# Scaling of normed tokens on ScalarE instead of VectorE, in a one-core macaron block

## The chip, the cores and the metric

The kernel runs on one core of a Trainium2 chip. The metric is device time in microseconds of one execution, given as the median of several runs; smaller is better.

## The reference

`x` has 4 batches of 512 tokens with 128 features. Three residual stages follow one another, each behind a layer norm over the 128 features:

```python
def _layernorm(x, axis=-1, eps=1e-05):
    m = jnp.mean(x, axis=axis, keepdims=True)
    v = jnp.var(x, axis=axis, keepdims=True)
    return (x - m) / jnp.sqrt(v + eps)

x = x + 0.5 * ffn(_layernorm(x), gate_w, Wg, Wu, Wd)
x = x + attn(_layernorm(x), Wa, ba, We, be, Wi, Wo, Wv, Wout, chi, beta_p, iv_p, ov_p)
x = x + 0.5 * ffn(_layernorm(x), gate_w, Wg, Wu, Wd)
```

`ffn` is a mixture of 8 experts in which every expert picks its 128 best tokens of a batch by a softmax over the gate logits; `attn` has 16 heads of 8 features, a softmax over the scores, and gates from two further projections of the normed tokens. Everything is float32.

## The kernel before

Tokens lie on the 128 partitions. `x` and `xn` hold 16 tiles of 128 tokens by 128 features: a batch `b` is 4 such tiles (`C = 4`, `B = 4`). The program is written by hand, one instruction queue for each engine; the order inside a queue is the order of the code, and engines release one another only by semaphores. An engine whose next instruction waits does nothing that stands behind it.

All three norms use the same parts, numbered `n` = 0, 1, 2. For each batch:

- VectorE, `norm_stats(n, b)`: four `bn_stats` and four `bn_aggr` give mean and variance of each token.
- ScalarE, `root(n, b)`: one square root of the four variances of each partition, with `norm_eps` as its bias, a tile of one column.
- VectorE, `norm_apply(n, b)`: one reciprocal (`rstd`), a wait for it, and four `tensor_scalar` that subtract the mean and multiply by `rstd` (L640).
- TensorE, `turn_xn(n, b)`: four transposes of `xn` into a PSUM bank (L956), each waiting for its own tile.
- ScalarE, `copy_xnT(n, b)`: one copy of that bank to `xnT` (L498).

In norm 0 VectorE does the statistics of batch `b` before `norm_apply` of batch `b - 1`. TensorE turns batch `b` and then makes the gate logits of batch `b - 1` (L963); `route` needs all four. GpSimd splits every `xn` batch in two float16 halves (L424, L426) for the gathers of the expert stages, in norms 0 and 2.

In norm 1 TensorE's order is: turn batch 0, `project_qk(0)` (L1103), turn batches 1 and 2, `project_vae(0)` (L1116), `project_qk(1)`, `project_vae(1)`, turn batch 3, `project_qk(2)`, `project_vae(2)`, and from there the row maxima of the scores (L1136, L810). The result of `project_qk` is kept as a high part, rounded by ScalarE (`copy_qk_hi`, L566), and a low part, the rest, by VectorE (`split_qk_lo`, L831). Both are stored to DRAM by SyncE (`store_parts`, L328) and loaded again as stacks (L335). There are two buffers of the parts, so batch `b` waits until the stores of batch `b - 2` have landed: ScalarE for the high ones, VectorE for the low ones. ScalarE's queue is `root(1, 0)`, `copy_xnT(1, 0)`, `root(1, 1)`, `copy_qk_hi(0)`, `root(1, 2)`, `copy_xnT(1, 1)`, `copy_xnT(1, 2)`, `root(1, 3)`, `copy_qk_hi(1)`, `copy_xnT(1, 3)`, `copy_qk_hi(2)` and so on. VectorE also adds the expert output to `x` (`add_moe`, L803) and the bias to the other projections (`add_bias`, L838).

In norm 2, the last heads of the attention are finished between the batches. TensorE's order is `turn_heads`, `turn_xn(2, 0)`, `turn_combined(3)`, `project_out(3)`, `turn_xn(2, 1)`, `logits(1, 0)` (which also waits for `x_attended`), `turn_xn(2, 2)`, `logits(1, 1)`, `turn_xn(2, 3)`, `logits(1, 2)`, `logits(1, 3)`.

Of the kernel before, what the change touches and what calls it, by code (L numbers as in the profile page):

```python
# [11 lines left out]
P = 128  # L12
F32 = mybir.dt.float32
# [5 lines left out]
ALU = mybir.AluOpType  # L19
ACT = mybir.ActivationFunctionType  # L20
# [27 lines left out]
def macaron_block(nc, x_in, Wa, ba, We, be, Wi, Wo, Wv, Wout, chi, beta_p, iv_p, ov_p, gate_w, Wg, Wu, Wd, out):  # L48
    B, S, D = x_in.shape
    H = Wa.shape[1]  # L50
    DH = D // H
    E, _, I = Wg.shape
    K = max(1, int(S / E * 2))
    C = S // P
    CL = C // 2
    T = B * C
# [13 lines left out]
    with ExitStack() as ctx:  # L70
        def sb(name, shape, dt=F32):
            return ctx.enter_context(nc.sbuf_tensor(name, shape, dt))
# [26 lines left out]
        x = sb("x", [P, T, D])  # L99
        xn = sb("xn", [P, T, D])  # L100
# [5 lines left out]
        mean_var = sb("mean_var", [P, T, 2])  # L106
        std = sb("std", [P, T])
        rstd = sb("rstd", [P, T])

        top = sb("top", [P, T])  # L110

# [81 lines left out]
        def by(n, name):  # L193
            return [sem(f"{name}{i}") for i in range(n)]


        dve_norm, var_ready, std_ready = by(3, "dve_norm"), by(3, "var_ready"), by(3, "std_ready")
        xn_ready, xn_turned, xnT_ready = by(3, "xn_ready"), by(3, "xn_turned"), by(3, "xnT_ready")

        pool_halves, halves_ready = by(2, "pool_halves"), by(2, "halves_ready")  # L200
# [21 lines left out]

        qk_projected, qk_hi_ready, qk_lo_ready = sem("qk_projected"), sem("qk_hi_ready"), sem("qk_lo_ready")

        hi_stored, lo_stored = ([by(2, f"{name}_stored{u}_") for u in range(2)] for name in ("hi", "lo"))
        vae_projected, vae_ready = sem("vae_projected"), sem("vae_ready")
        gate_exp_ready, gate_one_ready, gates_ready = sem("gate_exp_ready"), sem("gate_one_ready"), sem("gates_ready")
        swap_ready, wout_swapped, dve_rot, act_rot, rot_ready = (
# [56 lines left out]
        def _(sp):  # L285
# [34 lines left out]

            load_experts(0)
            def store_parts(b):
                for half, (parts, ready, stored) in enumerate(((part_hi, qk_hi_ready, hi_stored), (part_lo, qk_lo_ready, lo_stored))):
                    for qk in range(2):
                        blocks = parts_dram[qk, b].rearrange("h d (m n) t -> m n (h d) t", m=2)
                        sp.wait_ge(ready, 2 * b + qk + 1)
                        twice = blocks[half] if qk == 0 else blocks[:, half]
                        sp.dma_start(twice.rearrange("n r t -> r n t"),  # L328
                                     parts[:, b % 2, qk, :].bitcast(F32).unsqueeze(1).broadcast_to([P, 2, S])).then_inc(stored[b % 2][qk], 16)

            def load_stacks(b, g):
                for qk, stack in enumerate((q_stack, k_stack)):
# [17 lines left out]
                             k_rows_dram).then_inc(k_rows_filled, 16)  # L350
            store_parts(0)
            for qk in range(2):
                sp.wait_ge(hi_stored[0][qk], 16)
                sp.wait_ge(lo_stored[0][qk], 16)
            load_stacks(0, 0)
            store_parts(1)
            for g in range(1, G):
# [5 lines left out]
            load_max_rows(1, 1)  # L363
            for u in range(2):
                for qk in range(2):
                    sp.wait_ge(hi_stored[u][qk], 16 * B // 2)
                    sp.wait_ge(lo_stored[u][qk], 16 * B // 2)
            with sp.Fori(0, B - 1) as b:
                for step in range(1, G + 1):
                    n = b * G + step  # L370
# [119 lines left out]
        def _(act):  # L490
            def root(n, b):
                t = slice(b * C, (b + 1) * C)
                act.wait_ge(var_ready[n], C * (b + 1))
                nc.scalar.activation(std[:, t], mean_var[:, t, 1], ACT.Sqrt, bias=norm_eps[:]).then_inc(std_ready[n], 1)

            def copy_xnT(n, b):
                act.wait_ge(xn_turned[n], b + 1)
                nc.scalar.copy(xnT[:, b, :], ps[:, b, :]).then_inc(xnT_ready[n], 1)  # L498
# [53 lines left out]
            act.wait_ge(eps_made, 1)  # L552
            root(0, 0)
            for b in range(B):
                if b < B - 1:
                    root(0, b + 1)
                copy_xnT(0, b)
# [3 lines left out]
            def copy_qk_hi(b):  # L561
                for qk in range(2):
                    act.wait_ge(qk_projected, 2 * b + qk + 1)
                    if b >= 2:
                        act.wait_ge(hi_stored[b % 2][qk], 16 * (b // 2))
                    nc.scalar.copy(part_hi[:, b % 2, qk, :], ps[:, 4 + qk, :]).then_inc(qk_hi_ready, 1)  # L566

            def copy_max_rows(n, slot):
# [1 line left out]
                nc.scalar.copy(max_rows[:, slot, :], ps[0:HG * C, 7, 0:P]).then_inc(max_rows_ready, 1)  # L570

            root(1, 0)
            copy_xnT(1, 0)
            root(1, 1)
            copy_qk_hi(0)
            root(1, 2)
            copy_xnT(1, 1)
            copy_xnT(1, 2)
            root(1, 3)
            copy_qk_hi(1)  # L580
            copy_xnT(1, 3)
            copy_qk_hi(2)
# [5 lines left out]
            def copy_heads(n, slot):  # L588
                act.wait_ge(probs_used, n * C + 2 * C)
                act.wait_ge(heads_turned, n + 1)  # L590
                nc.scalar.copy(heads_out[:, slot, :], ps[:, 6, :]).then_inc(heads_copied, 1)
# [20 lines left out]
            for b in range(B - 1):  # L612
                root(2, b)
            copy_heads(B * G - 1, 1)
            copy_xnT(2, 0)
            copy_xnT(2, 1)
            root(2, B - 1)
            copy_xnT(2, 2)
            copy_xnT(2, 3)
            route(1)  # L620
            experts(1)
# [3 lines left out]
        def _(dve):  # L625
# [5 lines left out]
                for t in tiles:  # L631
                    nc.vector.bn_aggr(out=mean_var[:, t, :], in_=stats[:, t, :]).then_inc(var_ready[n], 1)

            def norm_apply(n, b, steps):
                t0 = slice(b * C, (b + 1) * C)
                dve.wait_ge(std_ready[n], b + 1)
                steps.did(nc.vector.reciprocal(rstd[:, t0], std[:, t0]))
                steps.settle()
                for t in range(b * C, (b + 1) * C):
                    nc.vector.tensor_scalar(xn[:, t, :], x[:, t, :], mean_var[:, t, 0:1], rstd[:, t:t + 1],  # L640
                                            ALU.subtract, ALU.mult).then_inc(xn_ready[n], 1)

            def rotation_angles(steps):

# [172 lines left out]
            for b in range(B):  # L817
                dve.wait_ge(x_loaded[b], 16)
                norm_stats(0, b, steps)
                if b > 0:  # L820
                    norm_apply(0, b - 1, steps)
            norm_apply(0, B - 1, steps)
            route(0)
            experts(0)

            def split_qk_lo(b):
                for qk in range(2):
                    dve.wait_ge(qk_hi_ready, 2 * b + qk + 1)
                    if b >= 2:
                        dve.wait_ge(lo_stored[b % 2][qk], 16 * (b // 2))  # L830
                    nc.vector.tensor_tensor(part_lo[:, b % 2, qk, :], ps[:, 4 + qk, :], part_hi[:, b % 2, qk, :].bitcast(F32),  # L831
                                            ALU.subtract).then_inc(qk_lo_ready, 1)

# [9 lines left out]
            for b in range(B):  # L843
                dve.wait_ge(x_added[0], b + 1)
                norm_stats(1, b, steps)
                if b < B - 1:
                    add_moe(0, b + 1)
                    norm_apply(1, b, steps)
                if b == B - 2:
                    split_qk_lo(0)  # L850
            norm_apply(1, B - 1, steps)
            dve.wait_ge(attention_consts, 1)
            add_bias(0)
            split_qk_lo(1)
# [77 lines left out]
            copy_combined(2)  # L932
            add_attention(2)
            norm_heads(B - 1, 2, steps)
            norm_apply(2, 0, norm_steps)
            norm_heads(B - 1, 3, steps)
            copy_combined(3)
            norm_apply(2, 1, norm_steps)
            add_attention(3)
            norm_apply(2, 2, norm_steps)  # L940
            norm_apply(2, 3, norm_steps)
            route(1)
            experts(1)
            for b in range(B):
# [344 lines left out]
```

## Time and profile before

| | |
|---|---|
| median of 3 runs | 482.74 us (482.29 to 483.13) |
| profiled execution, its own time | 482.52 us |
| its span in the profile | 480.8 us |
| TensorE matmul busy | 397.7 us, 83% |
| VectorE busy | 385.2 us, 80% |
| ScalarE busy | 232.2 us, 48% |
| GpSimd busy | 54.5 us, 11% |
| chain that ended last | TensorE 64%, VectorE 16%, ScalarE 4% |

The span leaves out 1.7 us around the profiled execution's work. Busy shares are averages over stages that have different limits: the three norms lie at about 4 to 20 us, 125 to 146 us and 355 to 372 us of the span, and what the change does is decided in those stretches.

### The profile page before, as it was taken

How to read it: one execution, taken by the hardware profiler on the slowest of the kernel's cores; microseconds unless marked ns; L12 is line 12 of the kernel's file. 1: busy time of each engine (PE TensorE's matmuls, PEld its weight loads, DVE VectorE, ACT ScalarE, POOL GpSimd, SP SyncE). 2: the span in 40 equal slices, each digit the busy share in tenths (PEclk: the TensorE clock that was granted, in tenths of full speed). 3: DMA queues.
4: the chain of work that ended last, by engine and by line, in shares of the span. 5: the costliest groups of instructions: out<-in, count | busy, mean ns of one | idle time of the engine just before them, and what ended most of it. 6: DMA issues, size and time to landing. Idle time of an engine off the chain costs nothing.

```text
span 480.8 us, 7695 instructions
## 1 busy us (share of the span) xinstructions
PE 397.7 (83%) x2204; PEld 213.2 (44%) x2204; DVE 385.2 (80%) x841; ACT 232.2 (48%) x439; POOL 54.5 (11%) x103
## 2 busy tenths in 40 slices
PE   2702999999778889999999999999977019999995
PEld 1600456776543543333333333334427004567764
DVE  6698957788789888999898899987546889577883
ACT  2400453432341157777777777778863003543322
POOL 4520002122000010000000000000014400011210
PEclk9999999999897669999999999999996558999998
DMA  6100002223069721111112111100200000022103
GB/s 178 46 0 0 1 1 67 65 58 92 4 237 287 274 79 46 45 46 46 44 49 56 60 49 52 44 1 2 67 1 0 0 1 1 1 65 65 41 25 89
DMA packets 25767, 27.48 MB, mean 57 GB/s; under 512 B 3920, under 2 KB 17488, under 8 KB 25680
## 3 DMA queue, kind: packets, MB, share of 16 engines
q1 hardware_dynamic: 25744, 27.20, 18.6%
q8 instruction: 12, 0.20, 0.2%
q14 instruction: 11, 0.09, 0.1%
HBM read 17.08 MB, written 9.98 MB: 56 GB/s over the span
## 4 chain that ended last, share of the span: by engine, by line
PE 64%; DVE 16%; issue 12%; ACT 4%; POOL 1%; DMA 1%; DVEq 0%; ACTq 0%; POOLq 0%
PE ps L1151 14%; PE ps L1161 13%; PE ps L1136 6%; PE ps L1038 5%; DVE probs L748 4%; DVE neg_max L810 3%; PE ps L1021 3%; PE ps L1053 3%; PE ps L1023 3%; PE ps L1054 3%; PE ps L1022 3%; ACT probs L599 2%; PE ps L963 2%; PE ps L1170 2%; DVE heads_out L709 2%
## 5 line engine op out<-in xcount | busy, mean ns | idle before, releaser
L810 DVE TENSOR_REDUCE neg_max<-ps 128x1 f32<-128x512 f32 x256 | 161.1, 681 | 14.3 <-PE ps L1136 14.2
L599 ACT ACTIVATE probs<-ps 128x512 f32<-128x512 f32 x256 | 136.8, 601 | 44.0 <-PE ps L1151 42.8
L1136 PE MATMUL ps<-stacks 63*128 63x512 f32 x256 | 105.7, 494 | 3.3 <-DVE neg_max L810 2.6
L1151 PE MATMUL ps<-stacks 64*128 64x512 f32 x256 | 95.0, 462 | 4.9 <-ACT probs L599 4.8
L1151 PEld LDWEIGHTS ps<-stacks 64*128 64x128 f32 x256 | 41.3, 190 | 76.3 <-ACT probs L599 65.7
L1161 PE MATMUL ps<-probs,v_ext 128*32 128x512 f32 x512 | 69.0, 612 | 0.0
L1136 PEld LDWEIGHTS ps<-stacks 63*128 63x128 f32 x256 | 43.8, 196 | 19.5 <-DVE neg_max L810 15.0
L525 ACT CAST stacks<-ps 128x512 fp32r<-128x512 f32 x32 | 17.2, 588 | 67.5 <-PE ps L1002 67.5
L771 DVE TENSOR_TENSOR vae_and_gates<-heads_out,ps 128x512 f32<-128x512 f32 x32 | 21.9, 686 | 21.3 <-ACT heads_out L533 19.3
L453 POOL TENSOR_TENSOR w_lo<-w_gu,w_hi 128x512 fp32r<-128x512 f32 x16 | 20.6, 1295 | 150.1 <-ACT w_hi L512 150.1
L748 DVE TENSOR_TENSOR probs<-slot_row,slot 128x1024 f16<-128x1024 f16 x32 | 36.5, 1219 | 0.1
L1002 PE MATMUL ps<-probs,xn_hi 128*128 128x512 f16 x64 | 26.2, 410 | 7.4 <-DVE probs L748 6.7
L537 ACT COPY down_out<-ps 128x512 f32<-128x512 f32 x16 | 9.4, 587 | 45.8 <-PE ps L1038 45.8
L1021 PE MATMUL ps<-stacks,w_hi 128*128 (+1 forms) x64 | 30.4, 475 | 1.1 <-ACT stacks L525 0.8
L1038 PE MATMUL ps<-vae_and_gates,wd_sb 128*128 128x512 f32 x64 | 30.5, 598 | 0.8 <-DVE vae_and_gates L771 0.8
L977 PE MATMUL ps<-ident,threshold_row 32*128 32x32 f32 x2 | 0.6, 310 | 33.4 <-DVE threshold_row L718 33.4
L478 POOL TENSOR_TENSOR v_ext<-vae_and_gates,expression 128x128 f32 (+1 forms) x16 | 6.5, 409 | 190.8 <-PE ps L1161 132.8
L763 DVE TENSOR_SCALAR place<-token_row,indexT 128x512 fp32r<-128x512 f32 x64 | 27.9, 499 | 0.0
L1053 PE MATMUL ps<-place,part_hi 128*128 128x512 f32 x64 | 26.5, 413 | 0.4 <-DVE part_hi L785 0.4
L533 ACT ACTIVATE heads_out<-ps 128x512 f32<-128x512 f32 x32 | 19.1, 598 | 15.3 <-PE ps L1023 13.6
L1002 PE MATMUL ps<-probs,xn_lo 128*128 128x512 f16 x64 | 26.3, 411 | 0.0
L1023 PE MATMUL ps<-stacks,w_lo 128*128 (+1 forms) x64 | 25.2, 394 | 0.0
(150 smaller groups left out, 539.2 us busy)
## 6 DMA issues: line engine op xcount, KB each, us to landing
stacks<-parts_dram SPq DMA_DIRECT2D x64, 128.0 KB, 2.4
parts_dram<-part_hi SPq DMA_DIRECT2D x8, 512.0 KB, 3.5
parts_dram<-part_lo SPq DMA_DIRECT2D x8, 512.0 KB, 5.8
w_gu<-in_L_ffn_Wg_dram SPq DMA_DIRECT2D x16, 128.0 KB, 2.1
w_gu<-in_L_ffn_Wu_dram SPq DMA_DIRECT2D x16, 128.0 KB, 2.2
wd_sb<-in_L_ffn_Wd_dram SPq DMA_DIRECT2D x16, 128.0 KB, 2.2
x<-in_L_attn_x_dram SPq DMA_DIRECT2D x4, 256.0 KB, 3.7
stacks<-k_rows_dram SPq DMA_DIRECT2D x2, 512.0 KB, 6.6
```

The costliest lines, as they stand in the source:

```text
L599: nc.scalar.activation(probs[:, u // HG, u % HG, :], ps[:, RING + ring_bank(step, u), :], ACT.Exp, scale=SCORE_SCALE).then_inc(probs_ready, 1)
L748: nc.vector.tensor_tensor(pick[:, b, c], slot_row[:].unsqueeze(1).broadcast_to([P, E, K]), slot[:, c, b * E:(b + 1) * E].unsqueeze(2).broa ...
L763: nc.vector.tensor_scalar(place[:, u, b, :], token_row[:], indexT[:, b, bass.ds(2 * i + o, 1)], None, ALU.is_equal).then_inc(place_ready[l ...
L810: nc.vector.tensor_reduce(neg_max[:, g, col, qt:qt + 1], ps[:, ring_bank(step, u), :], AX.X, ALU.max, negate=True).then_inc(max_taken, 1)
L1002: last = nc.tensor.matmul(ps[:, pick_bank(n) + k, :], half[:, C * b + c, :], pick[:, b, c, 4 * hf:4 * hf + 4, :], start=(c == 0), stop=(c ...
L1021: nc.tensor.matmul(ps[:, bank, :], w_hi[:, u, k, cols], tokens_hi, start=True, stop=False)
L1023: nc.tensor.matmul(ps[:, bank, :], w_lo[:, u, k, cols], tokens_hi, start=False, stop=True).then_inc(gate_up_done[l], 1)
L1038: last = nc.tensor.matmul(ps[:, 6, :], wd_sb[:, u, m, :], hidden[:, u, m, :], start=(m == 0), stop=(m == MI - 1))
L1053: nc.tensor.matmul(ps[:, b, :], wy_hi[:, u, b, :], place[:, u, b, :], start=False, stop=False, skip_group_check=True)
L1136: nc.tensor.matmul(ps[:, ring_bank(step, u), :], q_stack[rows, g, pp, chunk(qt)], k_stack[rows, g, pp, :], start=True, stop=True).then_inc ...
L1151: nc.tensor.matmul(ps[:, RING + ring_bank(step, u), :], k_stack[rows, g, pp, chunk(c)], q_stack[rows, g, pp, :], start=True, stop=True).th ...
L1161: last = nc.tensor.matmul(ps[32 * j:32 * j + 32, 6, :], v_ext[:, g, c, j, :], probs[:, c, j, :], start=(c == 0), stop=(c == C - 1))
```

## The change

VectorE's `norm_apply` becomes `norm_scale`: after the reciprocal, one small instruction makes `shift = -mean * rstd` for the four tiles of the batch. ScalarE's new `normalise(n, b)` then makes each tile as `rstd * x + shift`, with both as per-partition operands. `normalise` gets a place in ScalarE's queue in each norm, and some roots and copies there change places with it. Apart from that, the store of the high part and that of the low part of one buffer count on one semaphore, so that both must have landed before either part is written again, and SyncE waits once where it waited twice.

```diff
+        shift = sb("shift", [P, T])
...
+        scales_ready = by(3, "scales_ready")
...
-        hi_stored, lo_stored = ([by(2, f"{name}_stored{u}_") for u in range(2)] for name in ("hi", "lo"))
+        parts_stored = [by(2, f"parts_stored{u}_") for u in range(2)]
...
             for qk in range(2):
-                sp.wait_ge(hi_stored[0][qk], 16)
-                sp.wait_ge(lo_stored[0][qk], 16)
+                sp.wait_ge(parts_stored[0][qk], 32)
...
+            def normalise(n, b):
+                act.wait_ge(scales_ready[n], b + 1)
+                for t in range(b * C, (b + 1) * C):
+                    nc.scalar.activation(xn[:, t, :], x[:, t, :], ACT.Identity, bias=shift[:, t:t + 1],
+                                         scale=rstd[:, t:t + 1]).then_inc(xn_ready[n], 1)
...
             root(0, 0)
             for b in range(B):
+                normalise(0, b)
                 if b < B - 1:
                     root(0, b + 1)
                 copy_xnT(0, b)
...
                     if b >= 2:
-                        act.wait_ge(hi_stored[b % 2][qk], 16 * (b // 2))
+                        act.wait_ge(parts_stored[b % 2][qk], 32 * (b // 2))
                     nc.scalar.copy(part_hi[:, b % 2, qk, :], ps[:, 4 + qk, :]).then_inc(qk_hi_ready, 1)
...
             root(1, 0)
+            normalise(1, 0)
+            root(1, 1)
             copy_xnT(1, 0)
-            root(1, 1)
+            normalise(1, 1)
             copy_qk_hi(0)
             root(1, 2)
             copy_xnT(1, 1)
+            normalise(1, 2)
+            root(1, 3)
             copy_xnT(1, 2)
-            root(1, 3)
+            normalise(1, 3)
             copy_qk_hi(1)
             copy_xnT(1, 3)
             copy_qk_hi(2)
...
             copy_heads(B * G - 1, 1)
+            normalise(2, 0)
+            normalise(2, 1)
             copy_xnT(2, 0)
+            normalise(2, 2)
             copy_xnT(2, 1)
             root(2, B - 1)
             copy_xnT(2, 2)
+            normalise(2, 3)
             copy_xnT(2, 3)
...
-            def norm_apply(n, b, steps):
+            def norm_scale(n, b, steps):
                 t0 = slice(b * C, (b + 1) * C)
                 dve.wait_ge(std_ready[n], b + 1)
                 steps.did(nc.vector.reciprocal(rstd[:, t0], std[:, t0]))
                 steps.settle()
-                for t in range(b * C, (b + 1) * C):
-                    nc.vector.tensor_scalar(xn[:, t, :], x[:, t, :], mean_var[:, t, 0:1], rstd[:, t:t + 1],
-                                            ALU.subtract, ALU.mult).then_inc(xn_ready[n], 1)
+                nc.vector.scalar_tensor_tensor(out=shift[:, t0], in0=mean_var[:, t0, 0], scalar=-1.0, in1=rstd[:, t0],
+                                               op0=ALU.mult, op1=ALU.mult).then_inc(scales_ready[n], 1)
...
                     if b >= 2:
-                        dve.wait_ge(lo_stored[b % 2][qk], 16 * (b // 2))
+                        dve.wait_ge(parts_stored[b % 2][qk], 32 * (b // 2))
```

Every call of `norm_apply` becomes one of `norm_scale` in the same place of VectorE's queue.

## Rows read from the trace of the kernel before

**Rows 1.** The page: busy time of each engine, and the chain by engine.

```profile
PE 397.7 (83%) x2204; PEld 213.2 (44%) x2204; DVE 385.2 (80%) x841; ACT 232.2 (48%) x439; POOL 54.5 (11%) x103
...
PE 64%; DVE 16%; issue 12%; ACT 4%; POOL 1%; DMA 1%; DVEq 0%; ACTq 0%; POOLq 0%
```

**Rows 2.** Instructions that write xn: durations in ns, minimum, median, maximum.

```profile
L640 DVE TENSOR_SCALAR xn<-x,mean_var,rstd x48: 333/341/1315, 7.1 to 367.3; 128x128 f32<-128x128 f32 x48
```

**Rows 3.** Timeline of norm 0: start, duration, engine, line.

```profile
6.85 0.18 DVE L637 RECIPROCAL rstd<-std 128x4 f32<-128x4 f32 x1 [0.54 <-ACT std L494]
7.06 1.12 DVE L640 TENSOR_SCALAR xn<-x,mean_var,rstd 128x128 f32<-128x128 f32 x4
...
8.75 0.58 ACT L498 COPY xnT<-ps 128x512 f32<-128x512 f32 x1 [1.74 <-PE ps L956]
...
13.84 2.38 DVE L640 TENSOR_SCALAR xn<-x,mean_var,rstd 128x128 f32<-128x128 f32 x4
...
14.28 0.58 ACT L498 COPY xnT<-ps 128x512 f32<-128x512 f32 x1 [1.80 <-PE ps L956]
14.47 1.16 POOL L426 TENSOR_TENSOR xn_lo<-xn,xn_hi 128x512 f16<-128x512 f32 x1
...
20.00 0.29 DVE L688 TENSOR_REDUCE top<-ps 128x16 f32<-128x128 f32 x1 [3.78 <-PE ps L963]
```

**Rows 4.** Timeline of ScalarE: activations back to back, without and with a per-partition bias.

```profile
20.65 0.31 ACT L516 ACTIVATE expo<-shifted 128x128 f32<-128x128 f32 x1 [1.98 <-DVE shifted L690]
20.87 0.19 ACT L502 ACTIVATE hp<-head_params 128x3 f32<-128x3 f32 x1
20.96 0.19 ACT L503 ACTIVATE hp<-head_params 128x1 f32<-128x1 f32 x1
...
356.31 0.67 ACT L494 ACTIVATE std<-mean_var,norm_eps 128x4 f32<-128x4 f32 x3
```

**Rows 5.** ScalarE's group of roots: busy us, mean ns of one, idle before.

```profile
L494 ACT ACTIVATE std<-mean_var,norm_eps 128x4 f32<-128x4 f32 x12 | 3.2, 293 | 3.3 <-DVE mean_var L632 3.2
```

**Rows 6.** Timeline of norm 1 and of the maxima behind it.

```profile
127.80 1.11 DVE L640 TENSOR_SCALAR xn<-x,mean_var,rstd 128x128 f32<-128x128 f32 x4
...
129.98 2.07 PE L1103 MATMUL ps<-xnT,wi_sb 128*128 128x512 f32 x2 [0.68 <-ACT xnT L498]
...
131.84 1.66 PE L1103 MATMUL ps<-xnT,wo_sb 128*128 128x512 f32 x2
...
134.57 1.12 DVE L640 TENSOR_SCALAR xn<-x,mean_var,rstd 128x128 f32<-128x128 f32 x4
...
138.66 1.11 DVE L640 TENSOR_SCALAR xn<-x,mean_var,rstd 128x128 f32<-128x128 f32 x4
139.69 0.88 DVE L838 TENSOR_TENSOR vae_and_gates<-ps,bias_row 128x320 f32<-128x320 f32 x2
...
140.32 1.32 PE L1116 MATMUL ps<-wvae_sb,xnT 128*128 128x160 f32 x8 [1.44 <-DVE vae_and_gates L838]
...
146.64 0.58 ACT L566 CAST part_hi<-ps 128x512 fp32r<-128x512 f32 x1 [2.22 <-PE ps L1103]
...
155.70 0.68 DVE L831 TENSOR_TENSOR part_lo<-ps,part_hi 128x512 fp32r<-128x512 f32 x1
```

**Rows 7.** Two stretches of norm 1: busy time by engine, granted clock, DMA.

```profile
132.00:133.00 1.00, 1.00 (x3) 0.41 (x2) 0.96 (x8) 0.58 (x1) 0.00 (x0) 0.50 0.00 0
133.00:134.00 1.00, 0.94 (x5) 0.36 (x3) 0.69 (x3) 0.46 (x1) 0.00 (x0) 0.94 0.38 141
```

**Rows 8.** Timeline of SyncE's queue in norm 1 and behind it.

```profile
140.59 1.78 SPq L335 DMA_DIRECT2D stacks<-parts_dram  x4
...
143.47 2.27 SPq L328 DMA_DIRECT2D parts_dram<-part_lo  x2
```

**Rows 9.** Timeline of norm 2.

```profile
363.99 1.11 DVE L640 TENSOR_SCALAR xn<-x,mean_var,rstd 128x128 f32<-128x128 f32 x4
...
365.23 2.38 DVE L640 TENSOR_SCALAR xn<-x,mean_var,rstd 128x128 f32<-128x128 f32 x4
```

More of the change, by code:

```diff
@@ L322, in store_parts @@
             def store_parts(b):
-                for half, (parts, ready, stored) in enumerate(((part_hi, qk_hi_ready, hi_stored), (part_lo, qk_lo_ready, lo_stored))):
+                for half, (parts, ready) in enumerate(((part_hi, qk_hi_ready), (part_lo, qk_lo_ready))):
                     for qk in range(2):
@@ L328, in store_parts @@
                         sp.dma_start(twice.rearrange("n r t -> r n t"),
-                                     parts[:, b % 2, qk, :].bitcast(F32).unsqueeze(1).broadcast_to([P, 2, S])).then_inc(stored[b % 2][qk], 16)
+                                     parts[:, b % 2, qk, :].bitcast(F32).unsqueeze(1).broadcast_to([P, 2, S])).then_inc(parts_stored[b % 2][qk], 16)
             def load_stacks(b, g):
@@ L365, in _ @@
                 for qk in range(2):
-                    sp.wait_ge(hi_stored[u][qk], 16 * B // 2)
-                    sp.wait_ge(lo_stored[u][qk], 16 * B // 2)
+                    sp.wait_ge(parts_stored[u][qk], 32 * B // 2)
             with sp.Fori(0, B - 1) as b:
@@ L820, in _ @@
                 if b > 0:
-                    norm_apply(0, b - 1, steps)
-            norm_apply(0, B - 1, steps)
+                    norm_scale(0, b - 1, steps)
+            norm_scale(0, B - 1, steps)
             route(0)
@@ L847, in _ @@
                     add_moe(0, b + 1)
-                    norm_apply(1, b, steps)
+                    norm_scale(1, b, steps)
                 if b == B - 2:
                     split_qk_lo(0)
-            norm_apply(1, B - 1, steps)
+            norm_scale(1, B - 1, steps)
             dve.wait_ge(attention_consts, 1)
@@ L934, in _ @@
             norm_heads(B - 1, 2, steps)
-            norm_apply(2, 0, norm_steps)
+            norm_scale(2, 0, norm_steps)
             norm_heads(B - 1, 3, steps)
             copy_combined(3)
-            norm_apply(2, 1, norm_steps)
+            norm_scale(2, 1, norm_steps)
             add_attention(3)
-            norm_apply(2, 2, norm_steps)
-            norm_apply(2, 3, norm_steps)
+            norm_scale(2, 2, norm_steps)
+            norm_scale(2, 3, norm_steps)
             route(1)
```

## The prediction, made blind

> **What bounds the kernel now.** I read the page first, for the shares and the chain of the work that ended last [rows 1]. TensorE is busy 83% and VectorE 80%, ScalarE 48%, which invites the thought that work should go from VectorE to ScalarE. The reader should not stop there: the chain is TensorE for 64% and the norms are a few short stretches in it. So I went to the instructions that write `xn`, 48 of them at a median of 0.341 us [rows 2], and to the timeline of the three norms, which shows what happens around each batch of four.
>
> In norm 0 the first batch of four takes 1.12 us on VectorE and its copy `xnT` starts at 8.75 [rows 3]. The last batch takes 2.38 us instead of 1.12: one of its four instructions is the one of 1.3 us [rows 2], and it stands beside GpSimd's subtraction at 14.47 [rows 3]. So before, `xn` is complete at 13.84 + 2.38 = 16.22 us. TensorE then ends the last turn and makes the last logits, and `route` begins on VectorE at 20.00, as soon as they are there [rows 3]. From 16.22 to 20.00 nothing has slack, and in all of norm 0 TensorE runs at the pace of the turns, which wait for `xn`.
>
> In norm 1 the start is a chain through all engines: `xn` of batch 0 from 127.80, its copy, then `project_qk(0)` at 129.98 [rows 6]. `xn` of batch 2 comes at 134.57 and ends at 135.69. At 140.32 comes a different limit: TensorE had idled 1.44 us for VectorE's bias add at 139.69, which was late because VectorE was making `xn` of batch 3 from 138.66 [rows 6]. This is the place where relief of VectorE can pay. In norm 2 batches 2 and 3 of `xn` are the chain: from 363.99 and from 365.23, the latter again 2.38 us long [rows 9].
>
> **The price of one instruction.** Before: 0.34 us each and 1.12 us for four, a pace of (1.12 - 0.34) / 3 = 0.26 us. After: a ScalarE activation of 128x128 with two per-partition operands, of which the trace has none. The nearest row is `expo`, 128x128 from SBUF with constants: 0.31 us, and the next activation begins 0.87 - 0.65 = 0.22 us after it; the tiny one behind lets the next begin after 0.09 us [rows 4]. Of the operands the only row is `root`, whose bias is per partition: 0.293 us for 4 columns [rows 5] against 0.19 us for the tiny one, and three take 0.67 us, so (0.67 - 0.29) / 2 = 0.19 us of pace against 0.09 [rows 4]. One such operand costs 0.10 us, in duration and in pace alike. The second (the scale) has no row. I take it to cost the same: both are one value per partition to be fetched before the stream begins. That makes 0.51 us for one, a pace of 0.42 at most; I use 0.50 and 0.40, so four take 3 x 0.40 + 0.50 = 1.70 us. The bounds: if neither operand costs anything with 128 columns, four take 3 x 0.22 + 0.31 = 0.97 us; if the second is free, 1.33 us; if the second costs twice the first, about 2.1 us. I call the duration of four q and keep it in the sums.
>
> The Trainium skill has a figure for this that the trace can be held against ("ScalarE: Activation LUTs", section "What ACT_TABLE_LOAD costs"): 186 ns with immediates plus 0.833 ns a column, about 93 ns more for each per-partition operand, and about 93 ns of overlap between neighbours. By that an estimate is 479 ns for one and 1.64 us for four; `expo` and `root` agree with it within 0.02 us. The same page's "Rules for kernel authors" say to use VectorE for adds and multiplies, which speaks against the change; by its figure the sum below would be about 0.35 us smaller.
>
> VectorE's part that stays is the reciprocal, 0.18 us [rows 3], and one new small instruction, which I take at the reciprocal's price, 0.20 us with its wait: `xn` starts 0.2 us later than it did.
>
> **Norm 0.** ScalarE now makes a ring with TensorE: four `xn`, then the turn, then the copy, then the next four. The copy began 0.57 us after the last `xn` (8.18 to 8.75) and holds the engine about 0.49 us before the next can begin (its 0.58 less the 0.09 of overlap) [rows 3, 4]; with 0.02 for the wait a batch takes q + 1.08 us. The first starts at 7.27, so `xn` of batch 3 is complete at 7.27 + 4q + 3 x 1.08 = 10.51 + 4q. With q = 1.70 this is 17.31 against 16.22, +1.09 us. `root` stands between `xn` and the copy and hides in the 0.57. The statistics on VectorE come earlier, which buys nothing, since the ring waits for its own engine. The stall beside GpSimd goes away (ScalarE's copy at 14.28 keeps its 0.58 us while GpSimd works from 14.47 [rows 3]), and it is counted: 16.22 contains it. The break-even is q = 1.43. Below about q = 1.3 TensorE's own work sets the end, about 1.9 us earlier than now.
>
> **Norm 1.** `xn` of batch 0 starts at 127.99 and ends 0.78 us later than it did (129.69 against 128.91), so `project_qk(0)` starts at 130.76. It runs at half clock; the granted clock is 0.50 until 133 and 0.94 in the next microsecond [rows 7]. If the clock rises when it did, the four matmuls end at about 133.65 against 133.50 (131.84 + 1.66 [rows 6]), if it rises 0.78 later, at 134.30; call this E. Behind it on ScalarE stand `copy_qk_hi`, the root, `copy_xnT(1, 1)`, 0.49 + 0.19 + 0.49 us and small waits, then `xn` of batch 2: it ends at E + 2.92, that is 136.57 to 137.22 against 135.69. The turn of batch 2, `project_vae(0)` and `project_qk(1)` follow and end at 139.8 to 140.4 where they ended at 138.9. There the idle time of 1.44 us is waiting to be used: VectorE, without its four `xn`, has the bias ready by about 139.2, so TensorE goes on at once, at 139.8 to 140.4 against 140.32. `copy_xnT(1, 2)`, which now stands behind a root that waits for statistics, is ready near 138.8 and is not needed before 141.6. So norm 1 loses 0.1 us or gains 0.6: the gain on VectorE pays for the loss on ScalarE. I take 0, as the clock more likely follows the work.
>
> **Norm 2.** `xn` of batch 2 can start only when VectorE has its statistics: 364.19 instead of 363.99. Behind it on ScalarE stand `copy_xnT(2, 1)` (0.49) and the last root (0.30), then on VectorE the reciprocal and the shift (0.4), so batch 3 starts at 365.30 + q and ends at 365.30 + 2q = 368.70 against 367.61 (365.23 + 2.38 [rows 9]): +1.09. The break-even is q = 1.16. `copy_xnT(2, 0)` now stands behind `xn` of batch 1 and makes the logits of batch 0 begin some 0.5 us later, but TensorE then waits for the turn of batch 2 anyway, which hides this. TensorE's turn of batch 0 now ends where the turn of the last heads begins, which costs 0.05 at most.
>
> **The semaphores.** `copy_qk_hi(2)` now also needs the low parts of batch 0. They have landed at 140.59, since the stacks' load, which waits for both, is issued then [rows 8], and the copy is not due before 143: nothing. `copy_qk_hi(3)` needs the low parts of batch 1, issued from 143.47 over 2.27 us [rows 8], where its projection ends at 146.6 [rows 6]. It may wait some microseconds, but what follows needs it only at 155.7, when VectorE comes to `split_qk_lo(3)` after 16 maxima [rows 6]: nothing. Fewer waits on SyncE: nothing.
>
> **Sum.** 1.09 + 0 + 1.09 = +2.18 us on the span of 480.8, and the same on that execution's own 482.52. The median of the runs is 482.74, 0.22 above it; I forecast 482.74 + 2.18 = 484.9 us. What a measurement of this kernel tells from no change is about 0.2%, 1.0 us.
>
> **The rivals.** *The operands are cheap (faster).* One mechanism: the fetch of the second operand hides behind the first, or that of both behind the stream. It decides at q = 1.43 in norm 0. With q = 1.33 norm 0 gives -0.4, norm 1 -0.8 (the bias wait is used up fully), norm 2 +0.3: 481.8 us. With q = 0.97: -1.9, -1.4, -0.45: 479.0 us. For it: no row shows two operands. Against it: the one row of one shows 0.10 us at full. Chances 0.12 and 0.04.
>
> *The clock comes earlier (about the same).* In norm 1 TensorE recovers at 133.1 whatever the work does; then norm 1 gives -0.6, and norm 2's clock, half from 365, may cost or return as much. About 483.8 us and less. For it: the edge falls 3 us after the work began; against: one edge proves no fixed time. Chance 0.13.
>
> *A late store, or a table to be loaded for the new function.* If the low store of batch 1 landed after 155.7, each microsecond past it would count: up to 487. If the new function needed a table of its own, every root and every batch behind it would need a load again, and a single load is longer than a norm batch's slack: about 10 us. Copies run behind the roots without one. Chance 0.05 together.
>
> **How the numbers follow.** The forecast's case has 0.66; its own range is 483.7 to 486.4 (norm 1 from -0.6 to +0.9, q from 1.6 to 1.8). Slower by over 0.2% (above 483.7): 0.60 of it, 0.05 of the clock's case, 0.05 of the last, 0.70. Within 0.2%: 0.05, 0.07 and half of the 0.12, 0.17 in round numbers. Faster: the other half, the 0.04 and what is left, 0.13. For 8 in 10 the range goes from the rival with one cheap operand to a q of 1.8: 481.7 to 486.4.
>
> **What would show it.** The activation group at 0.48 to 0.51 us, four in 1.6 to 1.7; `route` of norm 0 starting near 21.1 instead of 20.00; the wait of TensorE on the bias add gone from norm 1; the first reduction behind norm 2 about 2.2 us later. The forecast is wrong if four take less than 1.4 us, or if the clock's edges shift stretches that I took as fixed.

## The result: slower, by more than forecast

| | median of runs | ratio to before, 95% interval |
|---|---|---|
| before | 482.51 us (481.76 to 483.13, 4 runs) | |
| changed | 486.85 us (485.35 to 489.06, 4 runs) | 1.0094 (1.0052 to 1.0136) |
| changed, run again | 486.06 us (485.07 to 487.57, 6 runs) | 1.0075 (1.0053 to 1.0096) |

The forecast was 484.9 us, with a range up to 486.4. The direction was right; the loss is +3.6 to +4.3 us where +2.2 was forecast. A ratio compares an edited kernel with the kernel before as it ran beside it (17 to 23 executions, medians of 482.22 to 482.61 us, from the last row of the table on), so the medians of two experiments below can be compared only to some tenths of a microsecond. The profiled execution of the changed kernel is the quickest of its four: 485.35 us, with a span of 483.6 against 480.8. The page of the changed kernel, busy times and granted clock in tenths, where [rows 1] has the busy times of before; the clock line of before follows:

```profile
PE 401.9 (83%) x2204; PEld 213.7 (44%) x2204; DVE 372.5 (77%) x805; ACT 250.4 (52%) x487; POOL 54.5 (11%) x103
...
PEclk9999999999888569999999999999996558999999
```

```profile
PEclk9999999999897669999999999999996558999998
```

VectorE lost 12.7 us of work and ScalarE gained 18.2; the span grew by 2.8. The two new kinds of instruction, durations in ns (minimum, median, maximum):

```profile
L499 ACT ACTIVATE xn<-x,shift,rstd x48: 477/482/497, 7.2 to 370.0; 128x128 f32<-128x128 f32 x48
```

```profile
L654 DVE SCALAR_TENSOR_TENSOR shift<-mean_var,rstd x12: 161/172/1011, 7.0 to 367.8; 128x4 f32<-128x4 f32 x12
```

The activation is at the forecast price, 0.48 us against 0.50. The small instruction has a median of 0.17 and a maximum of 1.01 us: this is the first thing that was not forecast.

**Where the time went.** I cut each profile at the same events: the first statistics, the first reduction of routing 0 (`top`), the first add to `x` in norm 1, the first row maximum, the table load of norm 2, the reduction of routing 1. Each number is the difference of two starts in the timelines.

| stretch | before | changed | difference |
|---|---|---|---|
| norm 0, to `top` | 16.15 | 16.93 | +0.78 |
| routing and experts 0 | 105.10 | 105.00 | -0.10 |
| norm 1, to the first maximum | 20.76 | 21.04 | +0.28 |
| maxima and attention | 209.15 | 208.90 | -0.25 |
| norm 2, to `top` | 16.38 | 18.60 | +2.22 |

Norm 0, timeline of the changed kernel, for [rows 3]: four activations take 1.65 us, the copy follows, and the ring has a period of 2.70 us: the three batches behind the first start 2.70 us apart, and the last at 15.28.

```profile
7.18 1.65 ACT L499 ACTIVATE xn<-x,shift,rstd 128x128 f32<-128x128 f32 x4 [0.44 <-DVE shift L654]
...
9.39 0.58 ACT L504 COPY xnT<-ps 128x512 f32<-128x512 f32 x1 [0.38 <-PE ps L970]
...
15.28 1.65 ACT L499 ACTIVATE xn<-x,shift,rstd 128x128 f32<-128x128 f32 x4
...
20.70 0.29 DVE L702 TENSOR_REDUCE top<-ps 128x16 f32<-128x128 f32 x1 [5.79 <-PE ps L977]
```

Norm 2, timeline, for [rows 9]. The reader is to see the `shift` instructions beside GpSimd's subtractions: the first starts at 364.62, while the subtraction of 364.00 runs until 365.15, and ends at 365.17; the second starts at 367.77 and ends at 368.78, with GpSimd busy from 367.61 to 368.76. ScalarE starts its four only then. The reciprocal at 364.43, which reads one tile, takes its 0.15 us beside the same subtraction. In the kernel before, the table load starts at 355.01 and the reduction at 371.39 (the last line below, from its timeline).

```profile
364.00 1.15 POOL L426 TENSOR_TENSOR xn_lo<-xn,xn_hi 128x512 f16<-128x512 f32 x1
...
364.43 0.15 DVE L652 RECIPROCAL rstd<-std 128x4 f32<-128x4 f32 x1
364.62 0.55 DVE L654 SCALAR_TENSOR_TENSOR shift<-mean_var,rstd 128x4 f32<-128x4 f32 x1
365.20 1.65 ACT L499 ACTIVATE xn<-x,shift,rstd 128x128 f32<-128x128 f32 x4 [1.49 <-DVE shift L654]
...
367.61 1.15 POOL L426 TENSOR_TENSOR xn_lo<-xn,xn_hi 128x512 f16<-128x512 f32 x1
367.77 1.01 DVE L654 SCALAR_TENSOR_TENSOR shift<-mean_var,rstd 128x4 f32<-128x4 f32 x1
368.81 1.65 ACT L499 ACTIVATE xn<-x,shift,rstd 128x128 f32<-128x128 f32 x4 [0.81 <-DVE shift L654]
...
374.24 0.29 DVE L702 TENSOR_REDUCE top<-ps 128x16 f32<-128x128 f32 x1 [5.46 <-PE ps L977]
```

```profile
371.39 0.29 DVE L688 TENSOR_REDUCE top<-ps 128x16 f32<-128x128 f32 x1 [3.78 <-PE ps L963]
```

Norm 1, timeline, for [rows 6]. The bias add starts at 139.50, ahead of the end of `project_qk(1)`, and `project_vae(1)` follows at 141.28 with no wait for VectorE: that part of the plan works. But `project_qk(0)` takes from 131.44 to 135.23, and ScalarE waits 3.90 us for a store before it can write the high parts of batch 3 (and 2.02 us more for the second of them, at 151.82). The low parts that need them are made from 156.60 on, so this wait is hidden.

```profile
131.44 2.08 PE L1117 MATMUL ps<-xnT,wi_sb 128*128 128x512 f32 x2 [0.68 <-ACT xnT L504]
...
133.31 1.92 PE L1117 MATMUL ps<-xnT,wo_sb 128*128 128x512 f32 x2
...
139.50 0.89 DVE L852 TENSOR_TENSOR vae_and_gates<-ps,bias_row 128x320 f32<-128x320 f32 x2
...
141.28 1.25 PE L1130 MATMUL ps<-wvae_sb,xnT 128*128 128x160 f32 x8
...
149.21 0.58 ACT L573 CAST part_hi<-ps 128x512 fp32r<-128x512 f32 x1 [3.90 <-DMA parts_dram<-part_lo]
```

Windows of the same stretch; the number behind the five engines is the granted clock (0.50 is 1.2 GHz, 1.00 is 2.4). Before, it fell at 129.7 and was full again at 133.1 [rows 7]; here it fell at 130.0 and is half until 136.8. First two windows of the kernel before, then three of the changed one:

```profile
129.00:130.00 1.00, 0.33 (x3) 0.13 (x2) 0.97 (x8) 0.58 (x1) 0.00 (x0) 0.86 0.00 0
130.00:133.00 3.00, 3.00 (x4) 1.37 (x5) 2.93 (x16) 0.88 (x2) 0.00 (x0) 0.50 0.00 0
```

```profile
130.00:131.00 1.00, 0.77 (x2) 0.24 (x2) 0.83 (x5) 0.62 (x3) 0.00 (x0) 0.50 0.00 0
134.00:136.00 2.00, 2.00 (x6) 0.89 (x4) 0.00 (x0) 0.88 (x3) 0.00 (x0) 0.50 0.47 183
136.00:137.00 1.00, 0.08 (x1) 0.00 (x0) 0.89 (x4) 0.93 (x4) 0.00 (x0) 0.60 0.41 158
```

### The profile page after: what moved, and what is told of

Its sections match the earlier page's. It is cut to its first block, busy times and chain, and to the rows that moved or that the text cites. A ratio compares the mean times of both kernels' runs of the same rounds, so it can differ in the third digit from the quotient of the medians.

```text
span 483.6 us, 7704 instructions
## 1 busy us (share of the span) xinstructions
PE 401.9 (83%) x2204; PEld 213.7 (44%) x2204; DVE 372.5 (77%) x805; ACT 250.4 (52%) x487; POOL 54.5 (11%) x103
## 3 DMA queue, kind: packets, MB, share of 16 engines
q1 hardware_dynamic: 25744, 27.20, 18.2%
## 4 chain that ended last, share of the span: by engine, by line
PE 65%; DVE 14%; issue 12%; ACT 6%; POOL 1%; DMA 1%; DVEq 0%; ACTq 0%; POOLq 0%
PE ps L1165 14%; PE ps L1175 13%; PE ps L1150 6%; PE ps L1052 5%; DVE probs L762 4%; DVE neg_max L824 3%; PE ps L1067 3%; PE ps L1068 3%; PE ps L1035 3%; PE ps L1037 3%; PE ps L1036 3%; ACT probs L610 2%; PE ps L970 2%; PE ps L977 2%; PE ps L1117 2%
## 5 line engine op out<-in xcount | busy, mean ns | idle before, releaser
L610 ACT ACTIVATE probs<-ps 128x512 f32<-128x512 f32 x256 | 136.8, 601 | 43.8 <-PE ps L1165 42.6
L453 POOL TENSOR_TENSOR w_lo<-w_gu,w_hi 128x512 fp32r<-128x512 f32 x16 | 20.7, 1299 | 149.8 <-ACT w_hi L518 149.8
L970 PE MATMUL ps<-ident,xn 128*128 128x128 f32 x48 | 16.0, 404 | 13.7 <-ACT xn L499 13.1
```

What stands on the lines that cost most here:

```text
L610: nc.scalar.activation(probs[:, u // HG, u % HG, :], ps[:, RING + ring_bank(step, u), :], ACT.Exp, scale=SCORE_SCALE).then_inc(probs_ready, 1)
L970: last = nc.tensor.transpose(ps[:, b, chunk(c)], xn[:, C * b + c, :], ident[:])
```

## The experiments

Theory A: the loss beyond the forecast comes from two things, the `shift` stalled beside GpSimd in norm 2, and a longer half-clock time of TensorE in norm 1. The rivals: it is scatter of the runs; the shared semaphore; ScalarE's longer queue as such.

**The same kernel again.** No edit.

> The changed kernel once more, nothing edited. Theory A (the profile of the first execution, span +2.8 us, is the whole loss): most executions lie 2.5 to 3.5 us above the kernel before, and the first runs that were higher were scatter. Theory B (something that varies from execution to execution adds to it, most likely TensorE's clock coming back later in one stretch): the median is 4 to 5 us above, and a profile of a slow execution shows one stretch 1.5 us or more longer than in the first profile, at a lower granted clock.

Measured: 486.06 us, ratio 1.0075 (1.0053 to 1.0096), and a profile with the same stretches (norm 1 21.05, norm 2 18.58). The loss is not scatter. Which of the two theories holds is not decided: +3.6 us lies between them, and the profile is of one of the quicker executions. The three with a mean granted clock of 0.927 took 485.07 to 485.76 us, the two with 0.922 took 487.56 and 487.57; but one of the first four executions, also with 0.927, took 487.03, so the mean clock is not the whole of the scatter.

**The semaphore alone.** Of the diff only the `parts_stored` lines; all `norm_apply` as before.

> Only the shared semaphore of the stores of high and low parts; all norms scaled on VectorE as before. If the added wait is hidden, as forecast: 0 us, within 0.5. If ScalarE's wait for the low parts of batch 1 (it ended only at 151.8 us in the changed kernel's profile) is felt later, +1 to +2 us, with the maxima or the first attention step starting later.

Measured: 482.26 us, 0.9989 (0.9974 to 1.0003). The added wait is hidden.

**One norm at a time.** The lines of `normalise`, its order and `norm_scale` for one norm, the other two as before:

```diff
-            normalise(2, 0)
-            normalise(2, 1)
             copy_xnT(2, 0)
...
-            norm_scale(2, 0, norm_steps)
+            norm_apply(2, 0, norm_steps)
```

> Norm 0 alone on ScalarE (and the shared semaphore). From the profile of the changed kernel: the first reduction of the routing starts 0.7 to 0.8 us later, so +0.8 us in total. If the phase of TensorE's clock is what a shift in norm 0 disturbs in later stages, the total is 2 us or more, or scatters by more than 2 us from run to run.

> Norm 2 alone on ScalarE (and the shared semaphore). The working of the prediction gives +1.1 us. The theory formed from the changed kernel's profile (the small shift instruction on VectorE stands 0.4 and 0.85 us longer beside GpSimd's subtraction, and both stand in the chain) gives +2.2 us, with two shift instructions of 0.5 us or more.

> Norm 1 alone on ScalarE (and the shared semaphore). The forecast's working gives 0, from -0.6 to +0.1 us: the loss on ScalarE is paid by the wait of TensorE on the bias add. The remainder of the runs so far (3.6 for all three, less 0.9 and 2.6) says +0.1. If the changed order on ScalarE were a loss of its own, +1 us or more. In the profile the wait of TensorE on the bias add should be gone.

Measured: norm 0 483.74 us, 1.0019 (1.0006 to 1.0033), that is +0.9; norm 2 485.36 us, 1.0053 (1.0033 to 1.0073), +2.6; norm 1 484.18 us, 1.0031 (1.0019 to 1.0043), +1.5. Norm 2 has its `shift` instructions at 0.55 and 1.01 us again and takes 18.60 us. Norm 1, forecast at 0, costs: its profile has 22.05 us for the stretch, and two half-clock times in it, 130.5 to 133.9 and 137.4 to 140.8. Three of its windows:

```profile
131.00:133.00 2.00, 1.97 (x3) 0.94 (x4) 1.30 (x7) 1.52 (x4) 0.00 (x0) 0.50 0.00 0
134.00:137.00 3.00, 1.54 (x7) 0.64 (x5) 1.67 (x6) 2.52 (x7) 0.00 (x0) 1.00 0.66 256
137.50:140.50 3.00, 3.00 (x10) 2.65 (x11) 1.81 (x9) 2.39 (x6) 0.00 (x0) 0.50 0.97 376
```

The profiles of all experiments, those below included, can be set side by side for norm 1. In the five without matmuls of zeros and with ScalarE's order in norm 1 (changed, run again, norm 1 alone, GpSimd held back, one operand) TensorE is at half clock for 6.8 us, once for 10.2, and the stretch takes 21.04, 21.05, 22.05, 22.14 and 22.71 us, 21.8 in the mean. In the five with VectorE's order (before, semaphore alone, norm 0 alone, norm 2 alone, GpSimd held back) it is at half clock for 3.4 us in each, and the stretch takes 20.76, 20.84, 20.06, 20.00 and 20.90 us, 20.5 in the mean. The difference is 1.3 us, near the +1.5 measured. It also matters what the half clock falls on: in the profiles of norm 0 alone and norm 2 alone it begins in the middle of `project_qk(0)` (132.3) or behind it (134.5), not ahead of it, and the stretch is as short as with full clock throughout (19.99, below).

**GpSimd's split held back**, in the changed kernel and in the one before:

```diff
-                    pool.wait_ge(xn_ready[2 * l], C * (b + 1))
+                    pool.wait_ge(xn_ready[2 * l], T)
```

> The changed kernel, with GpSimd's split of xn held back until all four batches of xn are there. Theory A (the small shift instruction of VectorE stands because of GpSimd's subtraction and this is 1.2 us of norm 2): the shift instructions take 0.16 to 0.18 us each, the stretch from the table load to the first reduction behind norm 2 falls from 18.6 to about 17.4 us, and the total is 1.2 us below the changed kernel, some 2.4 us above the one before. Theory B (it stands for another reason): it still takes 0.55 and 1.01 us, and the total does not move.

> The kernel before, with GpSimd's split of xn held back in the same way. If VectorE's four scalings of the last batch take 2.4 us only because of GpSimd, they take 1.1 us here, and norm 0 ends about 1.3 us and norm 2 about 0.5 us earlier, -1.8 us in total, less what GpSimd's late work costs VectorE or GpSimd in the routing behind (up to 1 us each). If the cause is another, 0.

Measured: `after_late` 486.88 us, 1.0101 (1.0084 to 1.0118). The stall is gone, as theory A says; the last two `shift` instructions of norm 2 are short, and it takes 17.41 us instead of 18.60, -1.2:

```profile
366.80 0.16 DVE L654 SCALAR_TENSOR_TENSOR shift<-mean_var,rstd 128x4 f32<-128x4 f32 x1
...
369.55 0.16 DVE L654 SCALAR_TENSOR_TENSOR shift<-mean_var,rstd 128x4 f32<-128x4 f32 x1
```

The total does not fall, though, and there my expectation of -1.2 us missed. The profile gives +1.3 us back in routing 0, +0.5 in routing 1 and +1.1 in norm 1, where the clock is half for 10 us (131.8 to 142.1). `before_late` measures 482.28 us, 1.0001 (0.9988 to 1.0015): no gain where -1.8 or somewhat less was expected. The four scalings of the last batch do take 1.12 us now instead of 2.38 [rows 3], and norm 0 is 0.73 us shorter; but GpSimd's work now meets the routing, and from the reduction of routing 1 to the end the profile takes 110.6 us instead of 109.4. Timeline of norm 0, and the chain in routing 1, where the product of two tiles (0.30 us in the kernel before) takes 0.90:

```profile
12.91 1.12 DVE L640 TENSOR_SCALAR xn<-x,mean_var,rstd 128x128 f32<-128x128 f32 x4
```

```profile
372.23 0.90 DVE affinity L696
```

**Only the last batch on ScalarE**, in each norm; batches 0 to 2 stay on VectorE.

```diff
+                if b == B - 2:
+                    normalise_last(0)
                 copy_xnT(0, b)
...
-            norm_apply(0, B - 1, steps)
+            scale_last(0, steps)
```

> The kernel before with only batch 3 of each norm scaled on ScalarE (in norm 1 behind the high parts of batch 1), the others on VectorE, two semaphores for the parts as before. If ScalarE's longer time for four (1.65 us against 1.12) is what costs and VectorE's stall and the bias wait are what can be saved, this takes the savings without the ring of ScalarE: norm 0 -0.5, norm 1 -0.8, norm 2 -0.5, together -1.8 us. If scaling on ScalarE costs wherever it is, it is slower than before by 0.5 us or more.

Measured: 484.29 us, 1.0036 (1.0022 to 1.0050), a miss. Norm 0 took 16.36 (+0.2) and norm 2 17.76 (+1.4), each with a `shift` stalled to 0.57 us beside GpSimd, and norm 1 21.92, with the clock half for 10 us. In norm 2 it fell to half at 361, 4 us earlier than before; in two experiments with matmuls of zeros below, with VectorE's order, such an early fall goes with a norm 2 that is 1.1 to 1.2 us longer. So this run does not tell what scaling the last batch on ScalarE costs by itself.

```profile
13.94 0.57 DVE L651 SCALAR_TENSOR_TENSOR shift<-mean_var,rstd 128x4 f32<-128x4 f32 x1
```

**One operand.** In norm 0 alone `scale=1.0`, a constant; the normed tokens of norm 0 are then not scaled, so other tokens are chosen.

> The changed kernel; in norm 0 alone the scale is the constant 1.0 and only the shift is a per-partition operand, so that the normed tokens of norm 0 are not scaled and the choice of tokens differs. If each operand costs the same, the next activation begins 0.29 us after the one before instead of 0.39, four take 1.27 us instead of 1.65, and norm 0 ends 1.1 us or more earlier than in the changed kernel (15.8 us or less from the first statistics to the routing, instead of 16.9), earlier than in the kernel before. If the second operand is free, nothing moves.

Measured: 486.19 us in its one run. Four activations take 1.28 us instead of 1.65, and norm 0 15.70 us instead of 16.93. The second operand costs (1.65 - 1.28) / 4 = 0.09 us each time, as much as the first; the forecast took 0.10. The rival with cheap operands falls, and norm 0 is shorter by 1.2 us, as expected if each operand costs the same. The total is no lower than the changed kernel's, since norm 1 takes 22.71 us in this execution, with two half-clock times.

```profile
7.22 1.28 ACT L499 ACTIVATE xn<-x,shift 128x128 f32<-128x128 f32 x4 [0.44 <-DVE shift L654]
```

**TensorE kept at work in norm 1.** Matmuls of zeros (float16, 128x512) into a bank that nobody reads; they add work and leave out none.

```diff
+            fill(7)
             turn_xn(1, 0)
+            fill(2)
             project_qk(0)
```

> The changed kernel with nine matmuls of zeros into an unused bank on TensorE in norm 1: seven in front of the turn of batch 0, two in front of project_qk(0). Theory A (norm 1 costs more in the changed kernel because TensorE idles longer for xn and stays at half clock for 7 us instead of 3.4): the granted clock stays full from 126 to 146 us, norm 1 takes 19.0 to 19.5 us instead of 21.0, and the total falls 1.5 to 3 us below the changed kernel. Theory B (it is ScalarE's longer queue): the clock may be full, but norm 1 keeps some 20.7 us or more.

> The kernel before with the same nine matmuls. By theory A norm 1 takes 19.0 to 19.3 us instead of 20.8 (project_qk(0) at full clock takes 1.8 us instead of 3.5), -1.5 us in total; with it, what is left between this and the changed kernel with the matmuls is norm 0 and norm 2, 2.9 us, and norm 1 differs by less than 0.3. By theory B the difference of the two in norm 1 is 0.8 us or more.

Measured: 485.40 us, 1.0059 (1.0039 to 1.0079), and 482.56 us, 0.9994 (0.9979 to 1.0010). The nine did not hold the clock in the changed kernel: it was half from 136.8 to 140.2, one wait later, and norm 1 took 20.68 us. In the kernel before they held it, and norm 1 took 20.00 us: 0.76 less, where I expected 1.5. Inconclusive between A and B, so I filled TensorE's next wait too: `fill(9)`, `fill(3)`, and `fill(4)` ahead of `turn_xn(1, 2)`.

> The changed kernel with sixteen matmuls of zeros on TensorE in norm 1: nine in front of the turn of batch 0, three in front of project_qk(0), four in front of the turn of batch 2, so that TensorE has work in each of its waits. Theory A (the clock is what norm 1 loses): full clock in all of norm 1, which takes 20.0 us or less, as much as the next kernel's. Theory B (ScalarE's queue costs by itself): at full clock norm 1 still takes 20.4 us or more, 0.4 us or more above the next kernel.

> The kernel before with the same sixteen matmuls in the same places of TensorE's queue. Norm 1 at full clock takes 20.0 us, as it did with nine. By theory A the changed kernel with these matmuls is level with it in norm 1, by theory B it is 0.4 to 0.8 us behind.

Measured: 484.01 us, 1.0047 (1.0031 to 1.0064), and 482.56 us, 0.9997 (0.9984 to 1.0009). Both have full clock in all of norm 1. Windows of the two (changed order first); the first maximum is at 145.33 and 145.32, and the first add to `x` at 126.34 and 125.33, so norm 1 takes 18.99 and 19.99 us:

```profile
126.00:146.00 20.00, 18.65 (x88) 11.04 (x87) 15.26 (x58) 14.57 (x33) 0.00 (x0) 1.00 0.49 178
```

```profile
125.00:145.00 20.00, 17.59 (x87) 10.52 (x85) 17.79 (x68) 8.67 (x17) 0.00 (x0) 1.00 0.48 169
```

Theory A holds, and more than that: at equal clock ScalarE's order is 1.0 us quicker in norm 1. The waits show where the time lies. With VectorE's order TensorE still idles for the bias add; with ScalarE's order it does not:

```profile
139.78 1.33 PE L1120 MATMUL ps<-wvae_sb,xnT 128*128 128x160 f32 x8 [1.43 <-DVE vae_and_gates L838]
```

```profile
139.86 1.25 PE L1134 MATMUL ps<-wvae_sb,xnT 128*128 128x160 f32 x8
```

In the kernel before, the total did not fall with norm 1, because norm 2 became longer: 17.46 us with nine matmuls of zeros and 17.60 with sixteen, instead of 16.38. The half clock of that stretch begins at 358.8 and 359.0 there instead of 365.2. The same window, before and with sixteen:

```profile
360.00:365.00 5.00, 3.26 (x23) 2.72 (x23) 4.84 (x20) 0.88 (x2) 1.77 (x2) 1.00 0.00 0
```

```profile
360.00:365.00 5.00, 4.42 (x20) 4.09 (x20) 3.93 (x17) 0.85 (x2) 1.77 (x2) 0.50 0.00 0
```

So an edit in norm 1 can go with other clock edges in norm 2, some 210 us later, and a total mixes both. Why the edge moved is not shown.

**Towards a better version.**

> The kernel before with matmuls of zeros in all three norms (10 in norm 0, 9 in norm 1, 12 in norm 2), to see whether this beats both kernels. If the clock rises by it in norm 0 (the logits there take 0.19 us each at half speed) and stays up in norm 2, norm 0 -1.5, norm 1 -1.5, norm 2 -1.5 us, together -4.5 us. If transposes and logits let the clock fall whatever stands in front of them, norm 0 and norm 2 stay and only the -1.5 of norm 1 is left.

> The kernel before with matmuls of zeros in all three norms and one behind each matmul of the first row maxima. If the half clock from 151 to 176 us is what makes the first attention step slow, the stretch from the first maximum to the first exponential stays at 22.7 us and the one behind it (186.3 us) falls by 1.5 to 2.5 us, for 478.5 to 479.5 us in total. If the first step is slow for another reason, or the extra matmuls delay the maxima, it stays at 481 us or goes above.

> Norm 1 alone on ScalarE, with the sixteen matmuls of zeros in norm 1 and twelve in norm 2, norms 0 and 2 scaled on VectorE: the version that the runs point to. If the parts add up, norm 0 takes 16.1 us, norm 1 19.0 instead of 20.8, norm 2 15.8 instead of 16.4, so -2.4 us on the profile and 480 to 480.5 us in the median, below both kernels. If the order of ScalarE gains in norm 1 only together with the shifted phase of the changed norm 0, norm 1 stays at 20 us or more, and the total at 481.5 or more.

`before_fill`: 481.22 us, 0.9973 (0.9964 to 0.9983), -1.3 us. Norm 0 did not move (16.14 us), norm 1 took 20.02, norm 2 15.75 instead of 16.38. `before_fill_max`, with one more matmul of zeros behind each of the first maxima: six executions from 486.04 to 494.31 us, ratio 1.0108 (1.0083 to 1.0134, without the two longest), a miss. The pairs of matmuls need 0.74 us each at full clock where VectorE needs 0.60, and 1.26 at half clock; the clock fell at 161 and stayed down for 27 us although TensorE was busy 26.38 of them:

```profile
161.00:188.00 27.00, 26.38 (x63) 11.29 (x64) 17.17 (x28) 5.38 (x11) 2.06 (x8) 0.50 0.42 156
```

`norm1_fill` scales norm 1 on ScalarE and norms 0 and 2 on VectorE, with the sixteen matmuls of zeros in norm 1 and twelve in norm 2: 481.01 us, 0.9971 (0.9961 to 0.9982). It beats both kernels, by less than the 2.1 to 2.6 us expected; norm 1 takes 18.99 us at full clock, norm 2 15.57, and the span is 478.6, 2.2 us below the one before. Over `before_fill`, which has no scaling on ScalarE, no gain is shown: 481.01 against 481.22 us, and spans of 478.6 and 478.4, since the microsecond gained in norm 1 is lost again in this pair of profiles (0.4 us in routing and experts 0, 0.6 in maxima and attention, 0.4 behind norm 2). Its window:

```profile
125.00:144.00 19.00, 17.57 (x82) 10.24 (x81) 14.60 (x57) 13.99 (x32) 0.00 (x0) 1.00 0.49 179
```

## Why the prediction was wrong, point by point

- **The price of one instruction** held: 0.48 us each, 1.65 for four, against 0.50 and 1.70, and 0.09 us for each operand. The figures of the Trainium skill ("ScalarE: Activation LUTs", section "What ACT_TABLE_LOAD costs") gave 479 ns and 1.64 us; the trace agrees within 0.01 us.
- **Norm 0** held as a mechanism, the ring of ScalarE: +0.78 on the profile and +0.9 in the run of norm 0 alone, against +1.09. The term was over-sized by q being 0.05 smaller, four times, and by a turn that closed 0.03 sooner in each batch. One thing beside it was wrong: below a q of about 1.3 the end was to come 1.9 us earlier. With one operand q is 1.28 and norm 0 is 15.70, 0.45 earlier than before; the ring, 10.51 + 4q, still sets it (-0.59) and would reach -1.9 only at a q of 0.95.
- **Norm 2** failed at the step "one new small instruction, which I take at the reciprocal's price": measured +2.22 instead of +1.09. The two instructions that lie on the chain took 0.55 and 1.01 us instead of 0.16, 1.24 us more together; 1.09 + 1.24, less 0.1 for the smaller q, is 2.23. That they stood because of GpSimd is shown by `after_late`, where they take 0.16 and norm 2 falls by 1.2; every profile with ScalarE's order there and GpSimd undisturbed has 18.58 to 18.60 us. The sign was in front of me: the stall of 1.3 us beside GpSimd [rows 2, 3] was counted as one that goes away, and not asked of the instruction that takes its place. The Trainium skill's "SBUF — State Buffer", section "🔬 SBUF: two separate sides", says that a VectorE operation with two SBUF inputs and a GpSimd operation that reads SBUF exclude one another for the whole instruction; the trace agrees: the two `shift` instructions end 0.02 us after GpSimd's, 4 columns in up to 1.01 us.
- **Norm 1** failed at the step on the clock: "if it rises 0.78 later" was taken as the worst. In the changed kernel TensorE was at half clock for 7 us (130.0 to 136.8) instead of 3.4, and in the other kernels with ScalarE's order for 6.8 to 10.2 us, or 3.4 with nine matmuls of zeros. The stretch took 20.7 to 22.7 us with it, with VectorE's order 20.0 to 20.9. The mechanism that the step argued, relief of VectorE pays the loss on ScalarE, was right and under-sized: at full clock it gains 1.0 us. With norm 1 alone the total is +1.5 us where I had 0. That the half clock is what costs is shown by the pair with sixteen matmuls; why ScalarE's order keeps the clock down longer stays open.
- **The rival with the clock** had the right place and the wrong sign: in the changed kernel the half-clock time was longer, not shorter. The rivals of a late store and of a table load fell: the semaphore alone is -0.1%, the wait of 3.90 us is real and hidden, and no load was added.
- **The sum**: with norm 0 at 0.78, norm 2 at 2.22 and norm 1 at the 1.3 us that the five profiles of each order give, it is 4.3 us, against 3.6 to 4.3 measured and 2.18 forecast. Either failed step alone, +1.1 in norm 2 or +1.3 in norm 1, would have left the time inside the range; together they pass its end at 486.4. The profile's 2.8 us is one execution with norm 1 at only +0.28. The single norms add up to 0.9 + 1.5 + 2.6 = 5.0 us, but their intervals (0.3 to 1.6, 0.9 to 2.1 and 1.6 to 3.5) are too wide to tell this from 3.6 or 4.3. What makes one execution of the changed kernel up to 4 us longer than another is not shown; no profile of a long one was taken. Two figures of the working were wrong without weight: the upper end of 486.4 needs norm 1 at +0.9 beside a q of 1.8, and with q = 0.97 norm 2 comes out at -0.37 by its own formula, not -0.45.

## What to carry to other kernels

Work moved off a busy engine pays only where that engine's lateness ends a wait; in a chain of one batch after another, price the ring that forms on the receiving engine (here 4 activations, turn, copy), not the sum of busy times. If a stall beside GpSimd disappears with an instruction, ask whether its replacement, however small, reads two SBUF tiles next to the same GpSimd work. Where TensorE has short idle times in a chain, look at where its clock falls and rises in several profiles of each kernel, not in one: with ScalarE's order, where the wait ahead of the turn of batch 0 is 2.17 us instead of 1.83 and the turns are slower, norm 1 was 1.3 us longer in the mean of five profiles, though at full clock it is 1.0 us shorter. That the length of that wait is the reason was not tested. A few matmuls of zeros in the gaps tell a cost of the clock from a cost of the order itself; before they are kept, the later stretches have to be looked at too, since here they took back in norm 2 what norm 1 had gained.

## What the runs showed of the hardware that was not expected

- A VectorE instruction of 128x4 elements took 0.16 us alone and up to 1.01 us beside a GpSimd subtraction of 1.15 us.
- The granted clock stayed at half with TensorE busy 3.00 of 3 us (norm 1 alone, 137.5 to 140.5) and 26.38 of 27 us (`before_fill_max`), so being busy in a stretch does not by itself show that the clock is full there.
- Matmuls of zeros in norm 0 did not shorten it: 16.14 us against 16.15. The clock column gives 1.00 there until 11.8 us and 0.50 from then on.
- The clock column of the early part of a profile is to be read with care: in the kernel before it gives 1.00 from 16.5 to 20.0 and 0.50 from 368.0 to 371.3, but the same sixteen logit matmuls take 3.42 us in both.
- Half clock of 3.4 us cost 0.8 us of norm 1 where it covered nearly all of `project_qk(0)` (20.76 us, with VectorE's order) and no more than 0.1 us where it began later (20.00 and 20.06, against 19.99 at full clock).
